# VectorE splits four of a tile's eight gelu slices between the two halves of the convolution

## The reference, cut to what matters

```
x = x + 0.5 * ffn(layernorm(x))        # h = gelu(x @ sign(w1).T * a1 + b1); out = h @ sign(w2).T * a2 + b2
x = x + attn(layernorm(x))             # below
x = x + 0.5 * ffn(layernorm(x))
# attn: xn = rms(x) * norm_w; x_branch, gate = split(xn @ W_in.T)
#       xc = silu(causal_conv4(x_branch) + conv_b)
#       dt = soft_clamp(softplus(xc @ W_dt.T + b_dt)); B, C = xc @ W_B.T, xc @ W_C.T
#       h  = h * exp(..dt*A..) + dt * B * xc   (2048 steps, norm clamp at every tenth), y = h . C + D * xc
#       return x + scale * ((y * silu(gate)) @ W_out.T)
```

## Time and profile before

| | before |
|---|---|
| median of 3 runs | 1534.88 us (1534.82 to 1535.24) |
| profiled execution, its own time | 1534.2 us |
| profiled execution, first to last instruction (span) | 1532.4 us |
| busy: PE, DVE, ACT, POOL | 1446.3, 1253.5, 1119.2, 941.0 us |
| mean granted TensorE clock | 0.991 of full speed |
| rounds 1 to 6 of the first stage, about | 85 to 384 us of the span |

### The profile page before, as it was taken

One profiled execution on the slowest core, in us unless ns is written; L12 is line 12 of the kernel. 1 busy time (PEld: TensorE's weight loads), 2 busy tenths in 40 slices (PEclk: granted clock), 3 DMA queues, 4 the chain that ended last, 5 costly groups with the idle time before them and its releaser, 6 DMA issues.

```text
span 1532.4 us, 25717 instructions
## 1 busy us (share of the span) xinstructions
PE 1446.3 (94%) x7022; PEld 1019.1 (67%) x7022; DVE 1253.5 (82%) x2526; ACT 1119.2 (73%) x2618; POOL 941.0 (61%) x956
## 2 busy tenths in 40 slices
PE   6999999999879999999999999999999998999998
PEld 5555555555467777777777777777666666677776
DVE  7776566745479999999999999999999999788884
ACT  4454455445999999999999999999999964334243
POOL 0224323432269999999999999999999998400000
PEclk9999999999999999999999999999999999999999
DMA  8224427444747666666657666566544347465520
GB/s 269 83 70 155 145 95 198 134 163 128 240 133 208 170 165 189 168 171 167 171 158 187 181 162 180 157 175 169 137 110 110 98 102 234 121 218 186 157 77 28
DMA packets 232326, 236.30 MB, mean 154 GB/s; under 512 B 46296, under 2 KB 198040, under 8 KB 232184
## 3 DMA queue, kind: packets, MB, share of 16 engines
q1 hardware_dynamic: 231240, 233.34, 52.9%
q10 hardware_dynamic: 944, 1.31, 0.2%
HBM read 136.31 MB, written 98.56 MB: 153 GB/s over the span
## 4 chain that ended last, share of the span: by engine, by line
DVE 35%; POOL 14%; PE 12%; issue 5%; DVEq 1%; POOLq 1%; DMA 1%; ACT 0%; SPq 0%; ACTq 0%
DVE h L1344 22%; POOL rc L1108 13%; DVE banks L1334 9%; PE banks L1493 4%; PE banks L1514 3%; PE banks L1524 3%; DVE qs L1328 2%; PE banks L1168 1%; DVEq L1342 1%; DMA ub<-scratch_ub 1%; DVE q_ln_st L1770 1%; DVE q_g L1679 1%; POOLq L1116 1%; DVE q_x L1651 1%; PE banks L1534 0%
## 5 line engine op out<-in xcount | busy, mean ns | idle before, releaser
L1344 DVE TENSOR_TENSOR_SCAN h<-decay,banks 128x352 f32<-128x352 f32 x820 | 710.4, 881 | 57.2 <-DVE banks L1334 2.9
L1119 POOL TENSOR_TENSOR hc<-h,bc 128x640 f32<-128x640 f32 x410 | 592.5, 1445 | 0.0
L1168 PE MATMUL banks<-hc,w_ident 128*128 128x320 f32 (+1 forms) x1664 | 525.7, 439 | 0.1
L1237 ACT ACTIVATE tb<-dtc,a 128x320 f32<-128x320 f32 (+1 forms) x832 | 417.5, 556 | 4.8 <-DVE x L611 4.8
L1168 PEld LDWEIGHTS banks<-hc,w_ident 128*128 128x128 f32 x1664 | 284.5, 191 | 70.2 <-issue 0.4
L1259 ACT ACTIVATE decay<-tb 128x640 f32<-128x640 f32 x410 | 295.2, 724 | 0.0
L1108 POOL TENSOR_TENSOR rc<-qs,w_mhalf 128x1 f32<-128x1 f32 x410 | 224.9, 549 | 107.0 <-DVE qs L1328 107.0
L1154 PE MATMUL banks<-ub 128*128 128x176 f32 x1640 | 272.2, 288 | 2.1 <-DMA ub<-scratch_ub 2.0
L1147 PEld LDWEIGHTS banks<-sc_ss,sc_ones 128*128 128x128 f32 x820 | 123.3, 189 | 158.1 <-ACT sc_sq L1248 151.3
L1154 PEld LDWEIGHTS banks<-ub 128*128 128x128 f32 x1640 | 216.4, 192 | 2.4 <-DMA ub<-scratch_ub 2.3
L1147 PE MATMUL banks<-sc_ss,sc_ones 128*128 128x1 f32 x820 | 151.6, 254 | 37.7 <-ACT sc_sq L1248 19.0
(11 more groups left out here) (133 smaller groups left out, 1812.5 us busy)
## 6 DMA issues: line engine op xcount, KB each, us to landing
ub<-scratch_ub SPq DMA_DIRECT2D x410, 107.5 KB
bc<-scratch_blk SPq DMA_DIRECT2D x205, 160.0 KB, 3.5
scratch_ub<-turned SPq DMA_DIRECT2D x64, 512.0 KB, 3.5
scratch_ub<-spread SPq DMA_DIRECT2D x64, 176.0 KB, 2.4
scratch_xc<-xc SPq DMA_DIRECT2D x8, 1024.0 KB, 4.8
scratch_sg<-sg SPq DMA_DIRECT2D x8, 1024.0 KB, 5.8
piece<-scratch_u SPq DMA_DIRECT2D x32, 256.0 KB, 4.0
q_ys<-scratch_y SPq DMA_DIRECT2D x8, 1024.0 KB, 5.6
```

Of the source, the lines that this page charges most:

```text
L1119: pool.tensor_tensor(hc[:, pl % 2, :, at * S:(at + 1) * S] .rearrange("p (c b n) e -> p c b n e", c=KE, b=B)[:, :, b], state(m)[:, :, 0:S] ...
L1168: mm = pe.matmul(banks[:, y_bank(p), 0:KE * B * wide], w.ident[:], rhs, start=(n == 0), stop=(n == N - 1))
L1237: act.activation(tanh_rows(c, r), dtc[:, c % 2, k * B:(k + 1) * B, 0:blocks_of(c) * S].rearrange("p b (k e) -> p k b e", e=S), ACT.Tanh, s ...
L1344: dve.tensor_tensor_scan(state(m).rearrange("p r e -> p (r e)")[:, half], decay[:, m % DRING, half], psI[m % B][:, half], 0.0, ALU.mult, A ...
```

## The change

`convolve` gets a second argument, the half that it does. The first half is issued as before, then the first four of the eight gelu slices are split, then the second half of the convolution is done with the halo copy behind it, then the last four slices are split. This holds in the rounds 1 to 6. Nothing is added or taken away: the number, the shapes and the operands of the instructions are the same on each engine, and only VectorE's order differs.

```
-        def convolve(i):
-            if i >= 1:
+        def convolve(i, part):
+            if i >= 1 and part == 0:
                 dve.wait_ge(xc_ready, 2 * i)
-            n = CONV * i
-            for c0 in range(0, KE, 2):
+            n = CONV * i + part * CONV // 2
+            for c0 in (2 * part,):
                 for tap in range(TAPS):
...
+            if part == 0:
+                return
             dve.wait_ge(conv_steps, n)
             dve.tensor_copy(xbuf[:, :, :, 0:TAPS - 1], xbuf[:, :, :, TT:]).then_inc(halo_done, 1)
...
-            convolve(i)
+            convolve(i, 0)
             if 1 <= i < LAST:
-                split_g(i + 1, 0, KH)
+                split_g(i + 1, 0, KH // 2)
+            convolve(i, 1)
+            if 1 <= i < LAST:
+                split_g(i + 1, KH // 2, KH)
```

## The result

| | before | changed |
|---|---|---|
| median | 1535.06 us (4 runs) | 1515.65 us (1512.32 to 1517.25, 4 runs) |
| ratio | | 0.9869, 95% interval 0.9851 to 0.9887 |
| profiled execution: own time, span | 1534.2, 1532.4 us | 1517.25, 1515.4 us |
| mean granted clock | 0.991 | 0.993 |

The changed kernel is 1.3% faster, 19.4 us by the medians. Two later groups of runs gave 0.9869 (0.9854 to 0.9884) and 0.9875 (0.9860 to 0.9889).

What follows compares the result with a forecast made beforehand. TensorE's queue was taken to set the pace in rounds 1 to 6. Gaps of 13.42 and slow clock of 5.10 us gave 18.5 us off 1534.2, so 1515.7, plus 0.7 for the median: 1516.4 us, range 1514.6 to 1522.

Steps and rivals of the forecast that it cites:

- The mechanism: Rounds 1 to 6: gelu 4 waits for VectorE's first split, so the gate projection waits for its PSUM bank.
- The gaps, 13.42 us: TensorE's idle time before the gate projection goes in all six rounds, 13.42 us in sum.
- The clock, 5.10 us: Gate projections of rounds 3, 5 and 6 lose their slow stretches, 3 x 1.70 us; bounds 0 and 5.10.
- The sum, 18.5 us: Rounds 1 to 6 save 13.42 us of gaps and 5.10 us of slow clock together.
- first case: Gap and slow clock both go: 1516.4 us, own range 1514.8 to 1518; chance 0.69.
- `down`'s cover, 0.8 us: In round 2 the eighth split ends 0.8 us before `down` needs slice 7, the thinnest cover in the chain.
- the added delay: GpSimd's cast and spreads falling on VectorE's splits: taken as 0 a round, bounds -1.1 to 3.6 us.
- The fifth case: Late second convolution half holds ScalarE's second `silu_xc` and followers; costs from 3.2 us of lateness, some 1544 us; chance 0.05.

Runs made afterwards that it cites:

- five-place kernel: The kernel before, VectorE's order untouched, with five places for gelu slices in `gf` instead of four; 1517.45 us, ratio 0.9888.
- the matmuls in the gap: The kernel before with two more, unused matmuls between `turn_xn` and the gate projection in rounds 1 to 6; 1527.5 us, ratio 0.9955.
- two-slice kernel: The changed kernel with two gelu slices instead of four split between the convolution's halves; 1523.55 us (0.9937), then 1524.31 us (0.9936).
- one-slice kernel: The changed kernel with one gelu slice instead of four split between the convolution's halves; 1532.42 us, ratio 0.9993.
- experiment with late splits: The changed kernel with three unused VectorE additions between the convolution's second half and the last four splits; 1523.91 us, ratio 0.9927.
- Held apart: The changed kernel with GpSimd's cast, subtraction and spreads held back until VectorE has done `low_x`; 1515.1 us, ratio 0.9873.
- eight-slice kernel: The changed kernel with all eight gelu slices split between the convolution's halves; 1513.14 us (0.9857), then 1513.89 us (0.9863).

## Why the prediction was right

- **The mechanism** held as put: one gap a round, from VectorE over four places of `gf` to the PSUM ring. The five-place kernel takes out the same wait in another way and gets most of the gain; one, two and four slices give it in doses.
- **The gaps, 13.42 us.** TensorE's idle time in the six rounds fell by 13.2.
- **The clock, 5.10 us.** All three slow stretches of these rounds went, and the matmuls in the gap brought 4.9 us by themselves. To take the upper bound was right for this kernel, since no gap is left that the clock could fall behind. How often it falls behind a gap that stays can't be told from the gap's length: the wait of 2.45 us in the two-slice kernel cost no clock, while three of 2.07 to 3.10 us in the one-slice kernel did, and a fourth of 2.08 us did not.
- **The sum, 18.5 us, was 1.1 us too small** for the stage (19.6). A round took 46.51 us and not 46.78. Back to back, the gate's matmuls follow the transposes after 0.87 us and not after the 1.03 that the row of `turn_xn` gives, and their group reads 7.03 us and not 7.13. I had subtracted the bracketed idle times, and a row's duration holds a little overlap that only shows where there is no gap. This is 0.25 to 0.27 us in each of rounds 1 to 5. In round 6 the saving was 0.2 us less than in the sum, since `down`'s wait took 0.45 us.
- **The time**, 1515.65 us against 1516.4, is in the first case's own range. The profiled spans differ by only 17.0 us. The other 2.6 of the stage's 19.6 were lost again: 1.6 near the scan's end, where the granted clock fell for longer in the run that was profiled (below), 0.8 little by little over the scan before that place, and 0.2 ahead of round 1. The medians differ by 19.4, but the changed kernel's four executions lie 4.9 us apart, so that the agreement with the forecast to 1 us is in part luck.
- **`down`'s cover, 0.8 us**, was thinner: 158.75 - 158.35 = 0.4 in round 2, and in round 6 a wait of 0.19. `down` starts 0.2 us earlier than I had it, and VectorE's splits end 0.2 later against the round. The experiment with late splits cost 9.7 us, nearly what the measured cover gives (9 to 11).
- **GpSimd.** I took 0 for the added delay, and by the rows it is so: the 1.1 us moved from the convolution to the second split (0.62 on its cast, 0.48 on its subtraction). They reach the gelus, the last of which ends 18.5 us behind `turn_zn` (149.75 - 131.24) and not 17.6 (150.5 - 132.91), but no bank of the gate projection waits for it. Held apart, VectorE gains them back, and the time stays.
- **The fifth case, slower**, had its point in the wrong place. I had given the second `silu_xc` 3.2 us of cover up to the first `scale_y`. But what TensorE needs is behind that: the first gate silu, for `project_dt`'s bank, and both `scale_y` with `tanh_v` between them, for `turn_y`. The second half of the convolution could come 4.3 us later (eight slices) with no loss, and 8.5 us later for 2.0 us a round, each counted from the round's `turn_zn`. So the cover is about 6.5 us (8.5 - 2.0, an estimate), and it would have had to be some 10 us late to make the kernel slower than before: 6.5, and the 3.3 us that a round has gained (19.6 / 6).

## What to carry to other kernels

- A ring shorter than the burst that fills it couples two engines through a third. Look what the reader of the ring does before it gets to its first slot: moving as many reads ahead as the burst needs can be enough. Here four were, two brought half of it (9.9 of 19.6 us), and one 1.3 us.
- A gap on TensorE can have a second price, the clock behind it. Look at the durations of the matmuls that follow, and not only at the idle time before them.
- A wait on an engine that works in order costs nothing until one of its followers is late for the engine that sets the pace. Walk the chain to each such place, also to the buffers that the followers free, and take the smallest cover. In the eight-slice kernel the first gate silu ends 3.6 us before `project_dt` wants its bank (159.40 against 162.96), and the second `scale_y` 2.3 us before `turn_y` (164.08 against 166.39).

## What the runs showed of the hardware

**The clock is not a function of the gap's length alone.** In the kernel before, two gaps of 2.67 and 2.68 us had nothing (round 2, granted clock 1.00 over the 4.7 us behind the gap) and 1.70 us (round 5, 0.65 over 4.9 us) behind them. In the one-slice kernel a gap of 2.10 us cost 1.7 us (round 2, granted clock 0.62 behind it) and one of 2.08 us nothing (round 5, 1.00), and in the two-slice kernel one of 2.45 us cost nothing (round 6, 1.00). The stay at the lower level, 1.2 GHz, cost the same each time, 1.70 us on the matmuls of a gate projection. What decides between two like gaps stays open.

**A part of the spread of the runs lies near the scan's end.** TensorE waits there once for a load of `ub`, in each profile. These rows are from the timeline of the changed kernel's second profile and from that of the eight-slice kernel:

```profile
1265.18 0.68 PE L1159 MATMUL banks<-ub 128*128 128x176 f32 x4 [2.32 <-DMA ub<-scratch_ub]
```

```profile
1263.37 0.68 PE L1157 MATMUL banks<-ub 128*128 128x176 f32 x4 [1.92 <-DMA ub<-scratch_ub]
```

The busy times of 30 us around it, in the changed kernel's first and second profile and in the eight-slice kernel:

```profile
1255.00:1285.00 30.00, 25.78 (x117) 18.13 (x116) 25.52 (x52) 13.50 (x38) 21.83 (x24) 0.89 0.79 218
```

```profile
1255.00:1285.00 30.00, 24.84 (x118) 17.05 (x116) 26.36 (x53) 14.34 (x40) 23.04 (x24) 0.94 0.76 224
```

```profile
1255.00:1285.00 30.00, 24.36 (x123) 16.51 (x122) 27.50 (x55) 14.91 (x42) 23.61 (x25) 1.00 0.80 236
```

The mean grant is 0.89, 0.94 and 1.00, and VectorE gets 52, 53 and 55 instructions through in the same time. The ten scan instructions there (line 1349, in the eight-slice kernel 1347, from the 791st to the 801st of the span) take 16.22, 15.15 and 13.89 us. So one and the same place, after like waits (2.17, 2.32 and 1.92 us), cost up to 2.3 us more in one execution than in another. This is part of the spread and not all of it. From `turn_zn` of round 7 to the end of the span it is 1151.3, 1149.9 and 1147.6 us in these three, and of the 2.2 us between the spans of the changed kernel's two profiles 1.1 lie at this place and 0.8 ahead of round 1. Neither kernel is free of it or alone with it. In the group where both kernels ran side by side, both profiles have 1149.2 us behind `turn_zn` of round 7, with the clock lowered in both. And 13 executions of the kernel before, in the first group of the experiments, lie between 1530.23 and 1537.87 us. What makes the clock fall in one execution and not in another stays open, and whether an earlier load of `ub` would end it wasn't tried.
